# First token block of a two-layer FFN kernel: one load split in two over both DMA queues, one warm-up matmul fewer

## The reference

```python
gate = lora_add(einsum('bnh,fh->bnf', x, W_gate), x, A_gate, B_gate)
up   = lora_add(einsum('bnh,fh->bnf', x, W_up),   x, A_up,   B_up)
act  = silu(gate) * up
y    = lora_add(einsum('bnf,hf->bnh', act, W_down), act, A_down, B_down)
nx   = y * rsqrt(mean(y * y) + 1e-5) * ln_w
g, u = einsum('bsh,ih->bsi', nx, gate_w), einsum('bsh,ih->bsi', nx, up_w)
x    = x + einsum('bsi,hi->bsh', silu(g) * u, down_w)
```

## Time and profile before

| | us |
|---|---|
| median of 3 runs | 397.51 |
| lowest and highest | 396.84, 397.71 |
| time of the profiled execution | 397.35 |
| its span, first to last instruction | 395.6 |
| TensorE busy | 392.0 |
| first warm-up matmul starts | 0.85 |
| first matmul on data (M1) starts | 4.29 |

### The profile page before, as it was taken

How to read it: one execution, slowest core, us unless ns; L and a number is a source line. 1 busy time by engine, 2 the same in 40 slices (tenths; PEclk the granted TensorE clock), 3 DMA queues, 4 the chain that set the end, 5 groups by cost and what they waited for, 6 DMA issues and landing times.

```text
span 395.6 us, 5733 instructions
## 1 busy us (share of the span) xinstructions
PE 392.0 (99%) x1984; PEld 327.2 (83%) x1984; DVE 314.7 (80%) x476; ACT 240.5 (61%) x386; POOL 10.6 (3%) x13
## 2 busy tenths in 40 slices
PE   9999999999999999999999999999999999999997
PEld 5899888888888888888888888888888888888885
DVE  4799979586836769578699787878787869899994
ACT  4979786867574469815745656464646494484740
POOL 6300000000000000000000000000000000000000
PEclk9999999999999999999999999999999999999999
DMA  7540243311111551000400021313130216005112
GB/s 271 177 138 0 83 131 102 107 53 55 53 55 54 162 160 53 2 0 0 161 0 1 10 99 55 106 53 108 58 121 37 89 57 236 18 2 199 54 55 106
DMA packets 14942, 32.42 MB, mean 82 GB/s; under 512 B 2370, under 2 KB 4930, under 8 KB 14914
## 3 DMA queue, kind: packets, MB, share of 16 engines
q1 hardware_dynamic: 13792, 30.22, 23.6%
q10 hardware_dynamic: 1122, 1.84, 1.3%
HBM read 29.95 MB, written 2.10 MB: 81 GB/s over the span
## 4 chain that ended last, share of the span: by engine, by line
PE 99%; DVE 0%; issue 0%; DVEq 0%
PE bank L1363 53%; PE bank L1699 17%; PE bank L1589 14%; PE bank L1507 3%; PE bank L1553 3%; PE bank L1542 3%; PE bank L1373 3%; PE bank L1611 1%; PE bank L1603 1%; PE bank L1501 1%; PE bank L1618 0%; PE bank L1708 0%; DVE act L1354 0%; DVEq L1352 0%
## 5 line engine op out<-in xcount | busy, mean ns | idle before, releaser
L1363 PE MATMUL bank<-xs,ws 128*128 128x512 f32 x840 | 195.1, 390 | 0.0
L1363 PEld LDWEIGHTS bank<-xs,ws 128*128 128x128 f32 x840 | 156.5, 188 | 32.0 <-issue 0.2
L415 ACT ACTIVATE xs<-act 128x512 fp32r<-128x512 f32 x71 | 42.8, 624 | 21.1 <-DVE act L1045 7.5
L1589 PE MATMUL bank<-xs,wdc 128*128 128x512 f32 x240 | 55.7, 390 | 0.0
L1589 PEld LDWEIGHTS bank<-xs,wdc 128*128 128x128 f32 x240 | 44.8, 188 | 9.4 <-issue 0.2
L889 DVE TENSOR_TENSOR xs<-act,xs 128x512 fp32r<-128x512 f32 x71 | 47.6, 686 | 2.7 <-ACT xs L415 2.1
L889 DVE TENSOR_TENSOR ws<-wraw,ws 128x256 fp32r<-128x256 f32 (+2 forms) x45 | 30.0, 669 | 13.1 <-ACT ws L415 13.0
L415 ACT ACTIVATE mu<-bank 128x512 f32<-128x512 f32 x44 | 26.1, 596 | 20.2 <-PE bank L1363 13.7
L1699 PE MATMUL bank<-xs,vs 128*128 128x512 f32 x168 | 38.2, 389 | 0.0
L415 ACT ACTIVATE bank<-bank 128x512 f32<-128x512 f32 x30 | 17.3, 580 | 34.3 <-PE bank L1363 33.4
L1699 PEld LDWEIGHTS bank<-xs,vs 128*128 128x128 f32 x168 | 31.5, 188 | 6.5
(11 more groups left out here) (133 smaller groups left out, 439.6 us busy)
## 6 DMA issues: line engine op xcount, KB each, us to landing
wraw<-wgu_in SPq DMA_DIRECT2D x22, 512.0 KB, 3.3
wdr<-vs_in SPq DMA_DIRECT2D x7, 512.0 KB, 3.5
wraw<-vj_in SPq DMA_DIRECT2D x3, 896.0 KB, 4.5
wdr<-wd_in SPq DMA_DIRECT2D x10, 256.0 KB, 2.8
xa<-xT_in SPq DMA_DIRECT2D x4, 256.0 KB, 4.3
xa<-xT_in ACTq DMA_DIRECT2D x2, 512.0 KB, 4.8
bgu_raw<-bgu_in SPq DMA_DIRECT2D x32, 32.0 KB, 1.9
xres<-xT_in SPq DMA_DIRECT2D x4, 256.0 KB, 3.0
```

Source lines behind the costliest of these rows:

```text
L415: return nc.scalar.activation(out_ap, in_ap, ACT.Copy, scale=scale)
L1363: ins = mm(z[:, :], w_slot(j)[:, w, s, k * P:(k + 1) * P], xs[:, c, r, k, :], start=(start and k == 0 and s == 0 and r == 0), stop=(k == 1 ...
L1589: ins = mm(z[:, :], wd[:, s, h * P:(h + 1) * P], x[r], start=(start and s == 0 and r == 0), stop=False, skip_group_check=True)
```

## The change

Token block 0 is loaded in two pieces of 256 columns (128 KB each) in place of one of 512. The first piece stays first on SyncE's queue, with a semaphore of its own, `s_x00_ld`. The second is issued by ScalarE, on its queue, directly behind the gate weights and ahead of the table touch, the up weights and the indices, and uses the semaphore that the whole block had. ScalarE waits for each piece before it copies that piece. WARM becomes 7.

```diff
-WARM = 8
+WARM = 7
...
+        s_x00_ld = sem("x_quarter_0_loaded")
...
-            for k in range(KT):
+            sp.dma_start(xa0[:, 0, 0:256], xT_in[0, 0, :, 0:256]).then_inc(s_x00_ld, 16)
+            for k in range(1, KT):
                 sp.dma_start(xa0[:, k, :], xT_in[0, k]).then_inc(s_x0_ld[k], 16)
-                if k >= 1:
-                    sp.dma_start(w0_raw[:, k], w0_in[k]).then_inc(s_w0_ld[k - 1], 16)
+                sp.dma_start(w0_raw[:, k], w0_in[k]).then_inc(s_w0_ld[k - 1], 16)
...
             nc.scalar.dma_start(w0_raw[:, 0, 0:256], w0_in[0, :, 0:256]).then_inc(s_w00_ld[0], 16)
+            nc.scalar.dma_start(xa0[:, 0, 256:CH], xT_in[0, 0, :, 256:CH]).then_inc(s_x0_ld[0], 16)
             a.wait_ge(s_warm, 2)
             silu(stat[:, 1:2], stat[:, 0:1]).then_inc(s_table, 1)
             nc.scalar.dma_start(w0_raw[:, 0, 256:CH], w0_in[0, :, 256:CH]).then_inc(s_w00_ld[1], 16)
...
+                if k == 0:
+                    a.wait_ge(s_x00_ld, 16)
+                    copy(xs[:, X11, 0, 0, 0:256], xa0[:, 0, 0:256]).then_inc(s_x00hi, 1)
                 a.wait_ge(s_x0_ld[k], 16)
                 if k == 0:
-                    copy(xs[:, X11, 0, 0, 0:256], xa0[:, 0, 0:256]).then_inc(s_x00hi, 1)
                     copy(xs[:, X11, 0, 0, 256:CH], xa0[:, 0, 256:CH]).then_inc(s_xhi[0], 1)
```

## The result

| | kernel before | changed kernel |
|---|---|---|
| median, 18 executions each (us) | 397.54 | 398.64 |
| lowest and highest | 396.82, 397.87 | 397.84, 399.71 |
| profiled execution: time, span | 397.35, 395.6 | 398.07, 396.3 |

The ratio of the times is 1.0033, with a 95% interval of 1.0024 to 1.0041: the change makes the kernel slower by some 1.3 us (the medians lie 1.1 us apart). The 18 times of the changed kernel fall in two groups: ten lie between 397.84 and 398.76 (median 398.08), eight between 399.01 and 399.71 (median 399.54). None of the 18 executions of the kernel before that ran beside them is over 397.87. The profiled execution belongs to the lower group.

What follows compares the result with a forecast made beforehand. TensorE, busy 392.0 of 395.6 us, was taken as the bound. Terms of -0.05 and +0.65 gave +0.6 us: 397.95 for the profiled execution, 398.1 as median, range 397.1 to 399.8.

Steps and rivals of the forecast that it cites:

- The sum: Whole kernel: -0.05 us for the first data matmul, +0.65 for late second piece and up weights, 0 otherwise: +0.6 us.
- the likeliest case's own range: Total time if the second piece is late without an effect on the pace: 397.6 to 398.5 us, chance 0.46.
- The likeliest outcome: Measured time against the kernel before: same within about 0.2%, 0.53; slower 0.41, faster 0.06.
- the later rise: Rival at TensorE's start: idle stretches delay the higher matmul pace; +1.8 us in the middle, 399.3, chance 0.27.
- M1: First data matmul on TensorE: starts near 4.2 us, bound by the gate weights, behind some 0.4 us idle; gain 0.05 us.
- Second token piece: Second load on ScalarE's queue: lands at 5.2 us, so matmul M3 starts at 5.69 instead of 4.85.
- my two bounds: Landing of the second 128 KB token load: 4.3 us, as fast as the gate weights, to 5.35, as the up weights.
- Up weights: Third load on ScalarE's queue: lands at 6.65 us, so matmul M9 starts at 7.15, 0.75 us later than before.
- two equal steps of 1.47 us: ScalarE's queue: the old distance from first to second landing, 1.47 us, taken again from second to third.
- Blocks 1 to 3, short weights, indices: Later loads: waits covered, cost nothing; without the cover of the short weights and indices, up to 1.4 us.

Runs made afterwards that it cites:

- warm7_only: Kernel before with its old loads and 7 warm-up matmuls instead of 8; ratio 1.0006 (0.9997 to 1.0015) against the kernel before.
- filled: Changed kernel's loads, 8 warm-up matmuls, three extra matmuls on ones in TensorE's idle stretches; ratio 1.0031 (1.0021 to 1.0042) against the kernel before.
- indices_second: Kernel before with only the 32-byte indices load moved ahead of the up weights on ScalarE's queue; ratio 1.0024 (1.0013 to 1.0035).
- late_up_issue: Kernel before, same load order, but ScalarE waits for GpSimd's second mask step before issuing the up weights; ratio 1.0024 (1.0011 to 1.0038).
- rows_split: Changed kernel's two load places, but token block 0 cut by rows of 2 KB, 8 warm-up matmuls; ratio 1.0040 (1.0028 to 1.0052) against the kernel before.
- before_warm4: Kernel before with its own loads and 4 warm-up matmuls instead of 8; ratio 1.0045 (1.0031 to 1.0059).
- warm4: Changed kernel with 4 warm-up matmuls instead of 7; ratio 1.0045 (1.0032 to 1.0058) against the kernel before, times 398.95 to 400.07 us.
- loads_only: Changed kernel's loads with all 8 warm-up matmuls; ratio 1.0033 (1.0020 to 1.0046) against the kernel before, times 398.10 to 399.04 us.
- two_contiguous: Changed kernel's two loads, each piece read from a contiguous 128 KB block in HBM, 8 warm-up matmuls; ratio 1.0030 (1.0017 to 1.0043) against the kernel before.
- one_load_1kb: Kernel before, its one load of token block 0 made of 256 rows of 1 KB from a copy in two contiguous pieces; ratio 1.0028 (1.0011 to 1.0045).
- piece_on_gpsimd: Changed kernel with the second token piece issued as GpSimd's first instruction; ratio 1.0037 (1.0019 to 1.0056) against the kernel before, times 397.70 to 401.42 us.
- both_on_sp: Changed kernel with the second token piece behind the first on SyncE's queue, 7 warm-up matmuls; ratio 1.0025 (1.0014 to 1.0035) against the kernel before.

## Why the prediction held, and where its steps failed

*The sum.* I predicted +0.6 us for the profiled execution, 397.95; it took 398.07, and the median of the lower group is 0.54 us above that of the kernel before. The median of all was predicted as 398.1 and is 398.64, inside 397.1 to 399.8 but above 397.6 to 398.5, the likeliest case's own range. The likeliest outcome, no change within 0.2% (0.53), was not what was measured: the ratio is above 1.002, on the side that had 0.41. The step that failed is the weight of the later rise, which got 0.27. It explains the eight times of the upper group, if they are what they look like, and these lift the median above the single sum; the 399.3 forecast for the middle of that rival is near their median of 399.54. One row was misread without consequence: 4.85 0.63 with x2 in the earlier trace rows is two matmuls of 256 columns and not the length of one. The pace ahead of M1 stands without it, as the last warm-up matmuls start at 2.94, 3.37 and 3.79.

*M1, wrong in this profile.* I had it near 4.2, as the gate weights would still share the engines with 2 KB packets. M1 started at 3.81: the gate weights were there at 3.4, not at 3.77. Packets moved from 2.0 to 2.8 us, by queue (packets, MB, share), first the changed kernel, then the kernel before:

```profile
q1 hardware_dynamic: 118, 0.11, 42.5%
q10 hardware_dynamic: 115, 0.11, 39.2%
```

```profile
q1 hardware_dynamic: 74, 0.15, 56.1%
q10 hardware_dynamic: 30, 0.03, 10.8%
```

The turns of both queues are equal once both are at work (118 and 115), as assumed. The Trainium skill (DMA: Bandwidth & Descriptors, "Queues, rings and completion order") says that each engine takes turns between its queues packet by packet. The equal counts agree. What I left out is the beginning: in the kernel before ScalarE's queue had got only 30 turns by 2.8 us, and now it got 115. That the smaller packets of the first piece are the reason fits, but is not shown, and one pair of profiles overstates it: in this profile of the kernel before nothing at all moved from 1.5 to 2.0 us, while 41 GB/s moved in `warm7_only`, whose loads are the same. The five other profiles with the block split by columns and read from its old place have M1 at 3.95 (`filled`), 4.03, 4.04, 4.11 and 4.26, so 3.81 is the earliest of six. The idle stretch ahead of M1 that I predicted isn't there in it.

*Second token piece, right in sign, too large.* Predicted 5.2 with M3 at 5.69, measured about 4.65 with M3 at 5.14. It was between my two bounds, not at the upper one.

*Up weights, right in number, wrong in reason.* Predicted 6.65 and M9 at 7.15; ScalarE got them at 6.59 and M9 started at 7.06. I reckoned with 128 KB in front on the same queue and with two equal steps of 1.47 us. The steps from one load's first use to the next were 1.26 (3.41 to 4.67) and 1.92 (4.67 to 6.59), so the sum came out right by luck. `indices_second`, with 32 bytes in front, and `late_up_issue`, with nothing, show the same delay: what counts is that the issue slips by 0.5 us. The delay it makes is larger than the slip, by a factor of about two and a half in the changed kernel (0.49 us of issue, 1.23 of landing). I didn't foresee that.

Where the 1.23 us come from can be read from the landings. Before, the up weights were issued ahead of weight block 1 (1.33 and 1.73) and landed ahead of it, ready for ScalarE at 5.36 and 5.96. In the changed kernel they are issued behind it (1.82) and land behind it, 4.8 us after their issue, where the block lands 4.7 us after its own. In all 14 profiles these two loads land in the order of their issue. So the up weights went from next to last to last of the first megabyte of loads, which is some 0.6 us (5.36 to 5.96), and that megabyte was complete another 0.6 us later (5.96 to 6.59), because the engines moved 110 GB/s less from 4 to 6 us: 0.22 MB, 0.6 us at 379 GB/s. This is an estimate, and the place in the order is not the cause by itself: in `rows_split` the up weights were issued ahead of weight block 1 (1.90 and 2.06) and came at 6.76 all the same.

*Blocks 1 to 3, short weights, indices: right.* M15 and everything behind it carry the shift of M9. The indices' loads began at 6.81 (I had 7.5), and ScalarE then waited 2.0 us and made the LoRA parts at 14.38 instead of 12.99, but TensorE came to `short(0)` later too and didn't wait for them.

*The pace.* That an idle stretch can hold the higher level back is shown by `before_warm4`, where nothing else was changed, and by `warm4`. The Trainium skill (TensorE: Matmul & The Clock Gate, "What's actually happening") says that the throttled state is the default and that activity releases it. Both runs agree in direction: with four warm-up matmuls the higher level came at about 8.4 and 9.8 us. That the changed kernel's upper group is this effect is likely but was not seen in a profile of one of its executions: the profiled one is of the lower group, and its higher level came no later than before. At 0.49 us lost for each us at the lower level, the 1.5 us between the groups would be a rise some 3 us later, an estimate.

The times of all kernels speak for it. Eight kernels show 0.5 us or more of idle TensorE at once ahead of M1 or M3 in their profiles (the changed one, `loads_only`, `rows_split`, `two_contiguous`, `one_load_1kb`, `piece_on_gpsimd`, `warm4`, `before_warm4`): 35 of their 76 times are at 399.0 or above. Five show at most 0.30 us there (`warm7_only`, `both_on_sp`, `filled`, `indices_second`, `late_up_issue`): 3 of 49, the one of 1408.58 left out. The last two are the closest comparison, as M9 is as late in them as in the changed kernel (7.12 and 7.25 against 7.06): 1 of 19 against 8 of 18. And the profiles of `piece_on_gpsimd` and `one_load_1kb` show executions of 401.42 and 399.41 us with the lower level kept to about 12 and 8.4 us. The groups were formed after the times were known, and the kernels differ in their loads too.

*What stays open.* Why the DMA engines moved less in the stretch from 4 to 6 us. The profiles fall in two sets: 379, 371 (`warm7_only`), 352 (`before_warm4`) and 393 GB/s (`one_load_1kb`) with the block in one load and the up weights issued by 1.36; 250 to 310 in nine kernels in which the up weights were issued later or the block was split, and 344 in `two_contiguous`. Packet size and the split itself are excluded as necessary causes (`rows_split`, `late_up_issue`). What makes the engines slower was not found, and half of the up weights' delay rests on it.

A version that beats both kernels was not found either. `both_on_sp` starts M1 at 4.11 and has the up weights by 4.64, but then waits for weight block 1; `piece_on_gpsimd` issues the up weights on time, but waits for the piece. In the kernel before, M1 has its inputs 0.1 us ahead, M9 and M15 some 0.6 and 0.7 us (the copies end at 5.78 and 7.11, the matmuls start at 6.41 and 7.79), and each version tried here with other loads made one of them late by more than that.

## What to carry to other kernels

When TensorE is busy throughout, read the start load by load: for each, the time of issue, of landing, and the first matmul that needs it, and ask of a split load what its second issue pushes back on the same queue, and which load of the other queue then goes ahead. Half a microsecond of issue time on a queue can be more than a microsecond of landing while the DMA engines are full. Count the idle time that a change puts ahead of the rise of TensorE's pace; it can cost more than the wait itself, in some executions and not in others, so look at all times and not at one profile.

## What the hardware showed that I had not expected

- A load that only was issued 0.73 us later (2.06 against 1.33) landed 1.4 us later, and the DMA engines moved 294 in place of 379 GB/s from 4 to 6 us.
- 1.7 us of idle TensorE ahead of M1 kept the lower level until about 8.4 us, with matmuls back to back from 4.42 on; in the kernel before it ended at about 5.7. In the slowest execution of `piece_on_gpsimd` it lasted until about 12 us.
- The granted clock of the windows view was 1.00 in stretches in which the starts lay 0.43 us apart. In the first microseconds the starts are what to go by.
